# Sync-queue loads moved behind the transposes, and fewer small VectorE instructions, in a latent-attention layer

## The chip, the cores and the metric

The kernel runs on one core of one Trainium2 chip. The metric is the device time of one execution in microseconds (us). The core has a matrix engine (TensorE, PE in the profile, with its weight loads as PEld), a vector engine (VectorE, DVE), an activation engine (ScalarE, ACT), GpSimd (POOL) and a sync engine (SyncE, SP) which in this kernel issues every DMA. Engines run their own instruction lists in order and wait for each other on counting semaphores.

## The reference

Input x is 2048 rows by 512. The layer is `x + attention(xn) + ffn(xn)`, where `xn` is x after a layer norm.

```
q = xn @ wq                          # 16 heads of 128 + 64 (rotary)
kva = xn @ wkv_a                     # 128 latent + 64 rotary columns
ckv = rmsnorm(kva[:, :128]) * kv_norm_scale
k_nope, v = split(ckv @ wkv_b)       # 16 heads of 128 and 128
q_pe, k_pe = rope(q_pe), rope(k_pe)  # one k_pe for all heads
scores = (q_nope . k_nope + q_pe . k_pe) * 192 ** -0.5, causal
out = softmax(scores) @ v @ wo
ffn = sum over 8 factors of xn @ factors[r], / sqrt(8), + bias
```

## The kernel before

Weights are absorbed: for a head, `wq` and the key part of `wkv_b` are multiplied once (`w_abs`, stored to DRAM), and so are the value part of `wkv_b` and `wo` (`w_vo`), so that scores are taken against the 128 latent columns and a head's output is one product more. Operands are split into a high and a low float16 part, and each product is three matmuls (high by high, high by low, low by high). The high part is a ScalarE copy and the low part a difference made on VectorE or GpSimd.

After a prologue (layer norm, transposes of x, latent keys; up to about 71 us of the profile) the work goes by units. A unit `i` is one head for one chunk of 512 query rows: 64 units, 16 heads for each of the chunks 3, 2, 1, 0 in this order, and two more rounds for what trails. A unit has four rows `r` of 128 queries, and a row has `chunk + 1` pieces of at most 512 keys, so each of units 0 to 15 has 16 pieces. All five instruction lists walk the same loops. For each piece:

- TensorE makes the scores (L534 to L540) in one of four PSUM banks. It may write a bank when ScalarE's exponential of four pieces before has read it.
- VectorE takes the maximum (L1123, L1125). After the row's last piece `row_max` makes the bias of the exponentials: L1135, then L1142, which computes `m * scale + head` in a `tensor_scalar` with two per-partition operands.
- ScalarE makes the exponential (L774, `exps`) and then a float16 copy of it, the high part (L784, `high_parts`).
- GpSimd makes the low part (L1341), and SP transposes both with one DMA (L1513).
- One unit later TensorE multiplies them by the latent values (L390 to L392).

Behind each row's pieces every engine does the row's `fills(i, r)`: the next unit's query, outputs of the unit before the last, and, in units 0 to 15 only, the weight work of heads to come. Of this weight work the following matters here.

- `load_wo(i)` (L1419) fills `wso`, which has one buffer. It is read by ScalarE's `sqo` fill of unit i at row 3 (L752, sum of squares). TensorE sums that over partitions (L439, fill `nv`) in unit i + 1, row 0, and VectorE's `scale_value` makes scales of the sum.
- `load_wq(i + 4)` (L1401) fills one of two buffers `wsq`, and `load_wk(i + 5)` (L1407) one of four buffers `wsk`. In odd units ScalarE squares both query weights of the pair i + 3, i + 4: `sq0` at row 2 and `sq1` at row 3 (L695). `sq1(i + 3)` therefore reads the `wsq` that `load_wq(i + 4)` fills in the same unit. TensorE's fill `nrm(i + 3)` (L439) comes in unit i + 1, row 0, behind `nv`, and waits for `sq1`. VectorE's `scale_pair` reads that.

The order on SP is written by hand in the loop at L1545. Within a unit at row 2 it is: `load_wo`, `load_wk`, `load_wq`; the row's transposes; `load_factor` (L1443, in units 1 to 7; in unit 0 four loads of L1438); `load_pe`. Rows 0, 1 and 3 have their transposes first and other loads and stores behind them. A transpose waits for GpSimd's low part of its piece.

In unit 0 alone, ScalarE's order is all exponentials of a row and then all its copies (L784). In the other units a copy follows each exponential but the first, one piece behind.

Of the kernel before, what the change touches and what calls it, by code (L numbers as in the profile page):

```python
# [6 lines left out]
F32, F32R = mybir.dt.float32, mybir.dt.float32r  # L7
# [5 lines left out]
P = 128  # L13
# [191 lines left out]
def build(nc, x, wq, wkv_a, wkv_b, wo, kvs, factors, bias, rope_t, rope_n, out):  # L205
    ctx = ExitStack()
    with ctx:
        def sb(name, shape, dt):
            return ctx.enter_context(nc.sbuf_tensor(name, shape, dt))
# [29 lines left out]
        nrf = sb("nrf", [P, KE], F32)  # L239
        lat = sb("lat", [P, 6], F32)  # L240
        fsc = sb("fsc", [P, 5], F32)
# [134 lines left out]
        def pair(i):  # L376

            return i % H // 2
# [259 lines left out]
        def _(e):  # L638
# [223 lines left out]
            for i in range(NU + 2):  # L862
                for r in range(QT):
                    last = chunk(i) if i < NU else -1

                    soon = last == 0 and r == 3 and i % 2
                    for kind, n in fills(i, r):
                        if soon and kind == "pv":
                            fill(kind, n)
                    for p in range(last + 1):  # L870
                        exps(i, r, p)

                        if p and i:
                            high_parts(i, r, p - 1)
                        if p == 2 and r < 2:

                            for kind, n in fills(i, r):
                                if kind in ("q", "wo", "parts", "sqv"):
                                    fill(kind, n)
                    for p in range(0 if i == 0 else max(last, 0), last + 1):  # L880
                        high_parts(i, r, p)
                    for kind, n in fills(i, r):
                        if soon and kind == "pv":
                            continue
                        if last < 2 or r >= 2 or kind not in ("q", "wo", "parts", "sqv"):
                            fill(kind, n)
# [3 lines left out]
        def _(e):  # L890
# [18 lines left out]
            def root(y, n):  # L909

                return e.tensor_scalar(y.bitcast(I32), n.bitcast(I32), -0.5, ROOT, ALU.mult, ALU.add)
# [4 lines left out]
            def scale_pair(i):  # L916
# [8 lines left out]
                e.wait_ge(z["v_fourth"], i // 2 + 1)  # L925
                e.tensor_scalar(t[:, 1:2], t[:, 2:3], lat[:, 4:5], None, ALU.add).then_inc(z["v_prod"], 1)
                root(t[:, 3:4], t[:, 0:1])
                e.wait_ge(z["v_prod"], i // 2 + 1)
                root(t[:, 4:5], t[:, 1:2]).then_inc(z["v_root"], 1)
                e.wait_ge(z["v_root"], i // 2 + 1)  # L930
                e.tensor_scalar(t[:, 5:6], t[:, 3:4], t[:, 4:5], None, ALU.mult)
                e.tensor_scalar(sc[:, 0:1], t[:, 3:4], WS, None, ALU.mult)
                e.tensor_scalar(sc[:, 1:2], t[:, 4:5], WS, None, ALU.mult).then_inc(z["v_w2"], 1)
                e.wait_ge(z["v_w2"], i // 2 + 1)
                e.reciprocal(t[:, 6:7], t[:, 5:6]).then_inc(z["v_inv"], 1)
                e.tensor_scalar(sc[:, 4:5], t[:, 5:6], lat[:, 5:6], None, ALU.mult).then_inc(z["v_tau"], 1)
                e.wait_ge(z["v_inv"], i // 2 + 1)
# [4 lines left out]
            def scale_value(h):  # L942
# [10 lines left out]
                e.wait_ge(z["v_nv"], h + 1)  # L953
                root(t[:, 2:3], t[:, 0:1])
                root(t[:, 3:4], t[:, 1:2]).then_inc(z["v_vroot"], 1)
                e.wait_ge(z["v_vroot"], h + 1)
                e.tensor_scalar(t[:, 4:5], t[:, 2:3], t[:, 3:4], None, ALU.mult)
                e.tensor_scalar(sc[:, 0:1], t[:, 2:3], WS, None, ALU.mult)
                e.tensor_scalar(sc[:, 1:2], t[:, 3:4], WS, None, ALU.mult).then_inc(z["v_vw"], 1)
                e.wait_ge(z["v_vw"], h + 1)  # L960
                e.reciprocal(sc[:, 2:3], t[:, 4:5]).then_inc(z["v_vsc"], 1)

            def scale_latent():
# [10 lines left out]
                e.reciprocal(lat[:, 2:3], lat[:, 3:4]).then_inc(z["v_lat"], 1)  # L974
                e.wait_ge(z["v_lat"], 1)
                e.tensor_scalar(lat[:, 5:6], lat[:, 2:3], WS * KS / RS, None, ALU.mult).then_inc(z["v_lat"], 1)

# [150 lines left out]
            def row_max(i, r):  # L1128
# [10 lines left out]
                if i < H and r == 0:  # L1139
                    e.wait_ge(z["v_scale"], i // 2 + 1)  # L1140

                e.tensor_scalar(nm[:, R % 4:R % 4 + 1], m, scales[:, pair(i), 3:4], head[:, 0:1], ALU.mult,  # L1142
                                ALU.add).then_inc(z["v_nm"], 1)

# [240 lines left out]
        def _(e):  # L1385
# [159 lines left out]
            for i in range(NU + 2):  # L1545
                k, h = divmod(i, H)
                for r in range(QT):
                    if r == 2:
                        if 1 <= i < H:
                            load_wo(i)  # L1550
                        if i + 5 < H:
                            load_wk(i + 5)
                        if i + 4 < H:
                            load_wq(i + 4)
                    if i < NU:
# [21 lines left out]
                    if 1 <= i and KE + (i - 1) * QT + r + 2 < NF:  # L1577
                        load_factor(KE + (i - 1) * QT + r + 2)
                    if r == 2 and i % 2 and H <= i + 3 < NU:
                        load_pe(i + 3)  # L1580
                    if r == 1 and h == H - 3 and k + 1 < NC:
# [48 lines left out]
```

## Time and profile before

| | |
|---|---|
| median of 3 runs | 1529.21 us (1527.36 to 1529.43) |
| time of the profiled execution | 1529.43 us |
| its span, first to last instruction | 1527.5 us |
| TensorE busy | 1479.1 us, 97% |
| VectorE, ScalarE, GpSimd busy | 66%, 64%, 59% |
| DMA engines of the core, moved | 73% busy, 226 MB on the one hardware queue |
| mean granted TensorE clock | 0.994 of full speed |

Times in the profile count from the first instruction of the span. The profiled execution took 1.9 us more than its span.

### The profile page before, as it was taken

The page shows a single profiled execution, that of the slowest core. Times are in us where ns is not written, and L with a number is a line of the kernel's source. Part 1 is how long each engine was busy: PE and PEld are TensorE (multiplying, and loading weights), DVE is VectorE, ACT ScalarE, POOL GpSimd, SP SyncE. Part 2 cuts the span into 40 slices and gives each one's busy share as a digit, 9 for nine tenths or more (in the row PEclk, how much of TensorE's full clock was granted, in tenths as well). Part 3 has the DMA queues.
Part 4 walks back from the last instruction along what each step waited for, and adds up shares of the span by engine and source line. Part 5 has one row for each costly group of instructions (what it writes and reads, how often), then busy time and mean ns, then how long its engine had stood idle before and what let it go on. Part 6 is the DMA issues. An engine that isn't in the chain of part 4 may idle for free.

```text
span 1527.5 us, 25754 instructions
## 1 busy us (share of the span) xinstructions
PE 1479.1 (97%) x7908; PEld 758.3 (50%) x7908; DVE 1012.5 (66%) x2563; ACT 974.4 (64%) x2418; POOL 904.7 (59%) x905
## 2 busy tenths in 40 slices
PE   5789999999999999999999999999999999999997
PEld 4444455555544544444445454545545555455553
DVE  6666777767777766655455565656656666676786
ACT  6777676777767476666466667665646666654553
POOL 1367777775655455666465656566645655664552
PEclk9999999999999999999999999999999999999998
DMA  6369989998776588787677677886856677854654
GB/s 219 105 124 206 205 181 189 187 189 163 150 154 139 114 174 168 142 175 138 131 143 139 134 139 146 153 162 134 155 117 138 136 140 149 157 133 98 120 119 99
DMA packets 646598, 227.83 MB, mean 149 GB/s; under 512 B 599360, under 2 KB 612160, under 8 KB 646080
## 3 DMA queue, kind: packets, MB, share of 16 engines
q1 hardware_dynamic: 646464, 226.20, 73.0%
q8 instruction: 65, 1.06, 0.3%
q14 instruction: 69, 0.57, 0.1%
HBM read 65.67 MB, written 17.83 MB: 55 GB/s over the span
## 4 chain that ended last, share of the span: by engine, by line
PE 80%; ACT 7%; DVE 6%; issue 3%; POOL 3%; DMA 1%; SPq 0%; POOLq 0%; ACTq 0%; DVEq 0%
PE ps L390 16%; PE ps L391 16%; PE ps L392 16%; PE ps L534 6%; PE ps L539 6%; PE ps L540 6%; PE ps L536 6%; PE ps L535 6%; ACT ex L774 3%; POOL st L1341 1%; DVE gm L1123 1%; DVE ps L1125 1%; POOL q L1332 1%; DMA st<-x_in 0%; ACT sqr L695 0%
## 5 line engine op out<-in xcount | busy, mean ns | idle before, releaser
L1341 POOL TENSOR_TENSOR st<-ex,st 128x512 f16<-128x512 f32 (+3 forms) x640 | 637.7, 1015 | 504.3 <-ACT st L784 494.5
L774 ACT ACTIVATE ex<-ps,nm,scales 128x512 f32<-128x512 f32 (+3 forms) x640 | 452.5, 709 | 466.8 <-DVE nm L1142 452.8
L1123 DVE TENSOR_REDUCE gm<-ps 128x1 f32<-128x512 f32 (+1 forms) x384 | 249.0, 669 | 176.8 <-PE ps L540 172.6
L784 ACT ACTIVATE st<-ex 128x512 f16<-128x512 f32 (+3 forms) x640 | 341.4, 561 | 5.9
L534 PE MATMUL ps<-kTh,q 128*128 128x512 f16 (+3 forms) x640 | 223.2, 349 | 8.5 <-ACT ex L774 8.4
L539 PE MATMUL ps<-kRh,q 128*128 128x512 f16 (+3 forms) x640 | 222.9, 348 | 4.5 <-POOL q L1332 4.5
L390 PE MATMUL ps<-pT,vH 128*128 128x512 f16 (+3 forms) x640 | 222.4, 347 | 2.4 <-DMA pT<-st 2.4
L536 PE MATMUL ps<-kTh,q 128*128 128x512 f16 (+3 forms) x640 | 223.0, 348 | 0.0
L535 PE MATMUL ps<-kTl,q 128*128 128x512 f16 (+3 forms) x640 | 223.0, 348 | 0.0
L540 PE MATMUL ps<-kRl,q 128*128 128x512 f16 (+3 forms) x640 | 223.0, 348 | 0.0
L391 PE MATMUL ps<-pT,vH 128*128 128x512 f16 (+3 forms) x640 | 222.5, 348 | 0.0
L392 PE MATMUL ps<-pT,vL 128*128 128x512 f16 (+3 forms) x640 | 219.3, 348 | 0.0
L1176 DVE SCALAR_TENSOR_TENSOR acc<-ps,rden,acc 128x512 f32<-128x512 f32 x256 | 189.7, 743 | 4.1 <-PE ps L392 3.7
L1332 POOL TENSOR_TENSOR q<-rot,q 32x512 f16<-32x512 f32 x128 | 149.0, 1164 | 28.6 <-ACT q L763 16.5
L1125 DVE CUSTOM_DVE_ANT_0 ps<-ps,cmask 128x256 f32<-128x256 f32 (+3 forms) x256 | 133.0, 519 | 26.1 <-PE ps L540 23.4
L774 ACT ACTIVATION_READ_ACCUMULATOR ex<-ps,nm,scales 128x1 f32 x640 | 125.7, 196 | 0.0
L1100 DVE SCALAR_TENSOR_TENSOR q<-ps,q 128x512 f16<-128x512 f32 x64 | 44.2, 691 | 114.6 <-ACT q L757 114.6
L390 PE MATMUL ps<-wV,oT 128*128 128x512 f16 x256 | 97.7, 382 | 4.7 <-issue 3.1
L534 PEld LDWEIGHTS ps<-kTh,q 128*128 128x128 f16 x640 | 62.7, 98 | 77.9 <-ACT ex L774 16.8
L391 PE MATMUL ps<-wV,oT 128*128 128x512 f16 x256 | 97.7, 382 | 0.0
L392 PE MATMUL ps<-wV,oT 128*128 128x512 f16 x256 | 97.7, 382 | 0.0
L390 PE MATMUL ps<-xT,wA 128*128 128x512 f16 x256 | 97.0, 379 | 0.0
(200 smaller groups left out, 2145.2 us busy)
## 6 DMA issues: line engine op xcount, KB each, us to landing
wA<-w_abs SPq DMA_DIRECT2D x48, 256.0 KB, 3.0
wV<-w_vo SPq DMA_DIRECT2D x48, 256.0 KB, 3.0
pT<-st SPq DMA_TRANSPOSE x640, 3.3
fland<-factors_in SPq DMA_DIRECT2D x28, 256.0 KB, 3.3
wP<-w_pe SPq DMA_DIRECT2D x24, 256.0 KB, 3.0
wsq<-wq_in SPq DMA_DIRECT2D x16, 256.0 KB, 3.9
wso<-wo_in SPq DMA_DIRECT2D x16, 256.0 KB, 3.1
w_abs<-wA SPq DMA_DIRECT2D x16, 256.0 KB, 2.3
```

Of the source, the lines that this page charges most:

```text
L390: e.matmul(o, a[0], b[0], start=first, stop=False)
L391: e.matmul(o, a[0], b[1], start=False, stop=False)
L392: return e.matmul(o, a[1], b[0], start=False, stop=last)
L534: e.matmul(b, q[:, i % 2, 0, qs], kTh[:, ks], start=True, stop=False)
L535: e.matmul(b, q[:, i % 2, 0, qs], kTl[:, ks], start=False, stop=False)
L536: e.matmul(b, q[:, i % 2, 1, qs], kTh[:, ks], start=False, stop=False)
L539: e.matmul(b, q[:, i % 2, 2, qs], kRh[:, ks], start=False, stop=False)
L540: e.matmul(b, q[:, i % 2, 2, qs], kRl[:, ks], start=False, stop=True).then_inc(z["p_s"], 1)
L774: e.activation(ex[:, n % NEX, 0:keys], s_bank(n)[:, 0:keys], ACT.Exp, bias=nm[:, (i * QT + r) % 4:(i * QT + r) % 4 + 1], scale=scales[:, p ...
L784: e.activation(stage(n, keys)[:, :, 0, :], ex[:, n % NEX, 0:keys].rearrange("p (t n) -> p t n", n=P), ACT.Copy).then_inc(z["a_pH"], 1)
L1123: e.tensor_reduce(m, b, AX_X, ALU.max).then_inc(z["v_max"], 1)
L1341: e.tensor_tensor(s[:, :, 1, :], ex[:, n % NEX, 0:keys].rearrange("p (t n) -> p t n", n=P), s[:, :, 0, :], ALU.subtract).then_inc(z["g_pL" ...
```

## The change

It has three parts.

1. SP: at row 2 of a unit, `load_wo`, `load_wk` and `load_wq` are issued behind the row's transposes and behind `load_factor`, no longer ahead of the transposes. `load_pe` keeps its place in the order.
2. ScalarE, unit 0: each high part is made one piece behind its exponential, as in the other units.
3. VectorE: in `scale_pair` and `scale_value` two operations on neighbouring columns become one on two columns, and operations with a per-partition scalar operand become ones between two tensors; `row_max` uses `scalar_tensor_tensor`, with one per-partition scalar operand and a tensor, where it used two scalar operands. One column of `lat` and its operation go.

```diff
@@ ScalarE
                         exps(i, r, p)
-                        if p and i:
+                        if p:
                             high_parts(i, r, p - 1)
...
-                    for p in range(0 if i == 0 else max(last, 0), last + 1):
-                        high_parts(i, r, p)
+                    if last >= 0:
+                        high_parts(i, r, last)
@@ scale_pair
-                e.tensor_scalar(t[:, 1:2], t[:, 2:3], lat[:, 4:5], None, ALU.add).then_inc(z["v_prod"], 1)
-                root(t[:, 3:4], t[:, 0:1])
+                e.tensor_tensor(t[:, 1:2], t[:, 2:3], lat[:, 4:5], ALU.add).then_inc(z["v_prod"], 1)
                 e.wait_ge(z["v_prod"], i // 2 + 1)
-                root(t[:, 4:5], t[:, 1:2]).then_inc(z["v_root"], 1)
+                root(t[:, 3:5], t[:, 0:2]).then_inc(z["v_root"], 1)
                 e.wait_ge(z["v_root"], i // 2 + 1)
-                e.tensor_scalar(t[:, 5:6], t[:, 3:4], t[:, 4:5], None, ALU.mult)
-                e.tensor_scalar(sc[:, 0:1], t[:, 3:4], WS, None, ALU.mult)
-                e.tensor_scalar(sc[:, 1:2], t[:, 4:5], WS, None, ALU.mult).then_inc(z["v_w2"], 1)
+                e.tensor_tensor(t[:, 5:6], t[:, 3:4], t[:, 4:5], ALU.mult)
+                e.tensor_scalar(sc[:, 0:2], t[:, 3:5], WS, None, ALU.mult).then_inc(z["v_w2"], 1)
...
-                e.tensor_scalar(sc[:, 4:5], t[:, 5:6], lat[:, 5:6], None, ALU.mult).then_inc(z["v_tau"], 1)
+                e.scalar_tensor_tensor(out=sc[:, 4:5], in0=t[:, 5:6], scalar=WS * KS / RS, in1=lat[:, 2:3],
+                                       op0=ALU.mult, op1=ALU.mult).then_inc(z["v_tau"], 1)
@@ scale_value
-                root(t[:, 2:3], t[:, 0:1])
-                root(t[:, 3:4], t[:, 1:2]).then_inc(z["v_vroot"], 1)
+                root(t[:, 2:4], t[:, 0:2]).then_inc(z["v_vroot"], 1)
                 e.wait_ge(z["v_vroot"], h + 1)
-                e.tensor_scalar(t[:, 4:5], t[:, 2:3], t[:, 3:4], None, ALU.mult)
-                e.tensor_scalar(sc[:, 0:1], t[:, 2:3], WS, None, ALU.mult)
-                e.tensor_scalar(sc[:, 1:2], t[:, 3:4], WS, None, ALU.mult).then_inc(z["v_vw"], 1)
+                e.tensor_tensor(t[:, 4:5], t[:, 2:3], t[:, 3:4], ALU.mult)
+                e.tensor_scalar(sc[:, 0:2], t[:, 2:4], WS, None, ALU.mult).then_inc(z["v_vw"], 1)
@@ row_max
-                e.tensor_scalar(nm[:, R % 4:R % 4 + 1], m, scales[:, pair(i), 3:4], head[:, 0:1], ALU.mult,
-                                ALU.add).then_inc(z["v_nm"], 1)
+                e.scalar_tensor_tensor(out=nm[:, R % 4:R % 4 + 1], in0=m, scalar=scales[:, pair(i), 3:4], in1=head[:, 0:1],
+                                       op0=ALU.mult, op1=ALU.add).then_inc(z["v_nm"], 1)
@@ SP
                 for r in range(QT):
-                    if r == 2:
-                        if 1 <= i < H:
-                            load_wo(i)
-                        if i + 5 < H:
-                            load_wk(i + 5)
-                        if i + 4 < H:
-                            load_wq(i + 4)
                     if i < NU:
                         for p in range(chunk(i) + 1):
                             transpose(i, r, p)
...
                     if 1 <= i and KE + (i - 1) * QT + r + 2 < NF:
                         load_factor(KE + (i - 1) * QT + r + 2)
-                    if r == 2 and i % 2 and H <= i + 3 < NU:
-                        load_pe(i + 3)
+                    if r == 2:
+                        if 1 <= i < H:
+                            load_wo(i)
+                        if i + 5 < H:
+                            load_wk(i + 5)
+                        if i + 4 < H:
+                            load_wq(i + 4)
+                        if i % 2 and H <= i + 3 < NU:
+                            load_pe(i + 3)
```

## Rows read from the trace of the kernel before

**Rows 1.** The page's busy time, share of the span and instructions of TensorE.

```profile
PE 1479.1 (97%) x7908; PEld 758.3 (50%) x7908; DVE 1012.5 (66%) x2563; ACT 974.4 (64%) x2418; POOL 904.7 (59%) x905
```

**Rows 2.** Windows: length, each engine's busy time, granted clock, DMA share, GB/s.

```profile
100.00:500.00 400.00, 396.29 (x2120) 200.78 (x2119) 292.94 (x752) 292.43 (x738) 282.07 (x269) 1.00 0.89 178
500.00:1500.00 1000.00, 998.32 (x5249) 502.87 (x5247) 640.07 (x1584) 603.59 (x1475) 586.08 (x578) 1.00 0.71 140
1500.00:1528.00 28.00, 17.36 (x85) 7.96 (x83) 14.90 (x35) 7.68 (x18) 5.12 (x6) 0.86 0.41 98
```

**Rows 3.** Waits of TensorE from 100 to 500 us: in total, times, longest.

```profile
PE ps L534 <- ACT ex L774: 3.5, 8, 0.9
```

**Rows 4.** Timeline of TensorE: the two longest of those waits, in brackets.

```profile
121.52 0.34 PE L534 MATMUL ps<-kTh,q 128*128 128x384 f16 x1 [0.68 <-ACT ex L774]
...
154.03 0.34 PE L534 MATMUL ps<-kTh,q 128*128 128x384 f16 x1 [0.92 <-ACT ex L774]
```

**Rows 5.** Timeline of SP, units 0 and 1: start, time in issuing.

```profile
100.11 0.39 SPq L1401 DMA_DIRECT2D wsq<-wq_in  x1
102.16 5.35 SPq L1513 DMA_TRANSPOSE pT<-st  x4
...
133.74 0.58 SPq L1443 DMA_DIRECT2D fland<-factors_in  x1
134.37 0.43 SPq L1419 DMA_DIRECT2D wso<-wo_in  x1
...
135.37 0.38 SPq L1401 DMA_DIRECT2D wsq<-wq_in  x1
135.80 5.58 SPq L1513 DMA_TRANSPOSE pT<-st  x4
```

**Rows 6.** Timeline of GpSimd: the low parts of unit 1, row 2.

```profile
131.29 4.26 POOL L1341 TENSOR_TENSOR st<-ex,st 128x512 f16<-128x512 f32 x4
```

**Rows 7.** DMA issues, us to landing: `wsq` of unit 1, then of unit 4.

```profile
wsq<-wq_in SPq DMA_DIRECT2D x1, 256.0 KB, 3.4
...
wsq<-wq_in SPq DMA_DIRECT2D x1, 256.0 KB, 4.7
```

**Rows 8.** Timeline of ScalarE: `sqo(1)` and `sq1(4)`, unit 1, row 3.

```profile
138.73 0.63 ACT L752 ACTIVATE sqs<-wso 128x512 bf16<-128x512 f32 x1
...
139.35 0.62 ACT L695 ACTIVATE sqr<-wsq 128x512 bf16<-128x512 f32 x1
139.87 0.20 ACT L695 ACTIVATION_READ_ACCUMULATOR sqr<-wsq 128x1 f32 x1
```

**Rows 9.** Timeline of TensorE: the product `nrm(4)`, unit 2, row 0.

```profile
140.38 0.36 PE L439 MATMUL ps<-nrm,ones 128*128 128x4 f32 x2
```

**Rows 10.** Timeline of TensorE: two waits in unit 0.

```profile
75.17 0.39 PE L539 MATMUL ps<-kRh,q 128*128 128x512 f16 x1 [3.01 <-POOL q L1332]
...
96.06 0.39 PE L534 MATMUL ps<-kTh,q 128*128 128x512 f16 x1 [1.60 <-ACT ex L774]
```

**Rows 11.** Windows behind those two waits, columns as in rows 2.

```profile
75.00:81.00 6.00, 4.72 (x17) 2.14 (x17) 2.86 (x7) 1.69 (x4) 0.12 (x1) 0.72 0.00 0
94.00:100.00 6.00, 4.40 (x28) 2.11 (x26) 5.54 (x11) 5.53 (x13) 5.70 (x6) 1.00 0.89 122
```

**Rows 12.** Small VectorE instructions by shape: count, busy us, mean ns, idle before.

```profile
L1142 DVE TENSOR_SCALAR nm<-rm,scales,head 128x1 f32<-128x1 f32 x192 | 52.4, 273 | 7.5 <-DVE rm L1135 0.6
...
L926 DVE TENSOR_SCALAR tot<-tot,lat 128x1 f32<-128x1 f32 x8 | 1.7, 214 | 0.3
L906 DVE SCALAR_TENSOR_TENSOR rstd<-mv,rstd 128x2 f32<-128x2 f32 x8 | 1.3, 160 | 0.3
...
L932 DVE TENSOR_SCALAR scales<-tot 128x1 f32<-128x1 f32 x8 | 1.1, 143 | 0.0
```

**Rows 13.** Timeline of unit 5: SP's transposes at row 2, `sq1(8)`, `nrm(8)`.

```profile
265.24 5.99 SPq L1513 DMA_TRANSPOSE pT<-st  x4
...
275.29 0.63 ACT L695 ACTIVATE sqr<-wsq 128x512 bf16<-128x512 f32 x1
...
277.11 0.36 PE L439 MATMUL ps<-nrm,ones 128*128 128x4 f32 x2
```

More of the change, by code:

```diff
@@ L239, in build @@
         nrf = sb("nrf", [P, KE], F32)
-        lat = sb("lat", [P, 6], F32)
+        lat = sb("lat", [P, 5], F32)
         fsc = sb("fsc", [P, 5], F32)
@@ L974, in scale_latent @@
                 e.reciprocal(lat[:, 2:3], lat[:, 3:4]).then_inc(z["v_lat"], 1)
-                e.wait_ge(z["v_lat"], 1)
-                e.tensor_scalar(lat[:, 5:6], lat[:, 2:3], WS * KS / RS, None, ALU.mult).then_inc(z["v_lat"], 1)
             def scale_factors():
```

## The prediction

> **What bounds the kernel now.** I read the page's busy times first. TensorE is busy 1479 of 1527.5 us [rows 1], so no other engine's time counts unless TensorE waits for it. The windows say where the 48 us that it isn't busy lie [rows 2]: 3.7 us between 100 and 500 us (most of units 0 to 15, in which the weight work is done), 1.7 us between 500 and 1500, 10.6 us at the end, and the rest, 32 us, ahead of 100 us. The waits of TensorE between 100 and 500 us are of one kind, for an exponential: 3.5 us in eight waits [rows 3]; the two longest are 0.68 and 0.92 us, one in unit 1 and one in unit 2 [rows 4]. The six others share 3.5 - 1.6 = 1.9 us. So the change can win little there, and what decides is whether it makes TensorE wait for something new.
>
> **Loads behind the transposes.** Issuing is slow on SP: four transposes take it 5.3 to 6.0 us [rows 5, 13], and a plain load of 256 KB some 0.4 to 0.6 us. In unit 1 SP is late: it goes from one transfer to the next without a pause from 133.74 to 141.38 us, while GpSimd's low parts of that row run from 131.29 to 135.55 us [rows 5, 6]. Here the moved loads lose the whole time of the row's transposes and of a factor load. Step by step, for `load_wq(5)`:
>
> - SP is done with the factor load of row 1 at 133.74 + 0.58 = 134.3 us. In the changed kernel it may be there sooner. In unit 0 it sits idle from 100.50 to 102.16 us with the next transposes waiting for GpSimd [rows 5], while two loads that now go behind are already out; and the earlier copies of unit 0 (below) bring the data sooner. Nothing shows how much comes of it: between 0 and 1.7 us. I take the middle, 0.9, and 133.4 us.
> - Four transposes, 5.6 us [rows 5]: 139.0. GpSimd is not in the way, its last low part is done at 135.6 [rows 6].
> - A factor load, 0.6, then `wso` and `wsk` at about 0.5 each: `wsq` is issued at 140.6 instead of 135.37.
> - It lands 3.4 us later as in unit 1 before, or 4.7 as in unit 4 [rows 7]. The transposes just ahead of it are still in flight, so I take 4.0: 144.6 us.
>
> Who waits? ScalarE reads it at 139.35 us for `sq1(4)` and needs 0.72 us to the end of it [rows 8]; now it ends at 145.3. Behind `sq1(4)` on ScalarE stand all the exponentials of unit 2. TensorE wants `sq1(4)` for `nrm(4)` at 140.38 us [rows 9], and behind that stand an output product and the scores of unit 2, row 1. So TensorE stops for about 4.9 us, nearly all of it lost, since nothing else is ready in its order. `wso`, issued 1 us sooner, lands and is squared before `wsq` is there and adds nothing. Bounds from the same rows: 133.4 - 0.8 and landing 3.4 give +3.5 us; no advance and landing 4.7 give +6.5 us.
>
> **The clock.** After the 3.01 us wait in unit 0 TensorE ran at the lower of its two levels (1.2 GHz instead of 2.4) for part of what followed: over 6 us the granted clock was 0.72, so 6 x 0.28 = 1.7 us of full-speed work were lost. After a wait of 1.60 us it stayed 1.00 [rows 10, 11]. A wait of 5 us is more like the first: +1.7 us, bounds 0 and 1.7.
>
> The Trainium skill, "TensorE: Matmul & The Clock Gate", Part 1, says that the gate halves the clock when the array has been idle and that the moment depends on a phase which runs free of the kernel, so it can fall otherwise from run to run. By it both 0 and 1.7 us are possible, and the row gives the likelier.
>
> **Later odd units.** Units 3, 5, 7, 9, 11 load a `wsq` that is read in the same unit, but there SP is not late. In unit 5 the transposes end at 271.23 us [rows 13]. Without three loads ahead of them they can start up to 1.4 us sooner; I take 0.9, as GpSimd holds them back. Then 270.3 + 0.6 + 1.0 = 271.9 for `wsq`, landing 275.3 to 276.6, and `sq1(8)` ends 0.72 later, 276.0 to 277.3. ScalarE wanted the data at 275.29, TensorE the sum at 277.11 [rows 13]. So ScalarE idles 0 to 1.3 us and TensorE 0 to 0.2. ScalarE's lateness goes into the exponentials and the query copy of the next unit, whose waits on TensorE are the small ones of [rows 3]. From unit 8 on there is no factor load, and it is nothing. In even units only `wso` is late, and `nv` comes late enough on TensorE. With TensorE set back by unit 1, SP has caught up by unit 2.
>
> **VectorE's small instructions.** L1142 takes 273 ns with two per-partition operands, L926 214 with one, L932 143 with none [rows 12]: some 65 ns each. A `scalar_tensor_tensor` with one such operand isn't in this trace at that size; L906, with a constant and two tensors, takes 160 [rows 12]. So the new L1142 lies between 160 and 273 ns; nearest is 160 plus one operand, 214 to 225. I take 214: 59 ns a row, 256 x 59 ns = 15 us of VectorE, all of it beside a busy TensorE, and 0.06 us on the path to an exponential where one is waited for. `scale_pair` loses two operations of 143 ns, of which I count half, since neighbours without a wait between them overlap, and about 0.06 three times: 0.3 us (bounds 0 and 0.5). `scale_value` likewise 0.2. These stand ahead of the maxima in rows 0 and 1, and so in the chain that ends the waits of [rows 3]: up to 0.5 us for an even unit, 0.25 for an odd one. Of the 1.9 us of the six small waits I take 1.0 back, the rest being eaten by the late `sq1`. The 0.92 us wait of unit 2 goes whole, for TensorE comes there later than the exponentials do: it lost 4.9 + 1.7, they lost 4.9 less 0.5. The 0.68 us of unit 1 may shrink, but lies ahead of the new stop, whose end SP sets; so a gain there, or in the prologue or unit 0, only makes the stop longer, and counts nothing.
>
> **Unit 0's copies.** They put one copy in front of the third exponential of a row and two in front of the fourth. TensorE's waits there end with the first exponential of a row [rows 10], which they leave alone. Bounds -0.3 and +0.5 us; whatever it is, the stop in unit 1 swallows it, apart from SP's advance above. If that stop isn't there, they are worth about -0.2.
>
> **The sum**, against the profiled execution's own 1529.4 us (0.2 above the median, at the top of the three runs): stop +4.9, clock +1.7, wait of unit 2 -0.9, small waits -1.0. That is +4.7, and 1534.1 us. The end of the kernel, 10.6 us of idle, has two rows of L1142 in its chain at most, -0.1, which I leave out.
>
> **The rivals.**
>
> - A, the loads are hidden anyway, and the kernel isn't slower. It needs `wsq` in place by 139.7 us, so the issue done by about 136, where 140.6 is my figure. It decides if the four transposes take SP 1 us in place of 5.6, or SP comes 5 us sooner. The Trainium skill, "DMA: Bandwidth & Descriptors", Issuing engines are not separate DMA queues, calls the issuing time usually small beside the transfer, which speaks for A. The rows speak against it: 5.58 us of issuing for four, back to back. What A gives: -0.9 -1.9 -0.2 and some 0.3 of the 0.68, 1526.1 at best; with half of it, 1528.
> - B, as forecast, but the clock keeps its level: the wait of unit 2 then shrinks by 0.5 only, +4.9 - 0.5 - 1.0 = +3.4, 1532.8.
> - C, the lateness repeats: in units 3, 5 and 7 `wsq` lands at the slow end or beyond. Each then costs 0.2 of TensorE's own waiting and up to 1.3 through late exponentials, and the 1.0 isn't won: +1.0 + 3 x 1.0 = 4 us more, 1538. For it: the DMA engines are 89% busy [rows 2]. Against it: landings in 3.4 to 4.7 us already under that load.
> - D, partly hidden: SP is 2 us or more ahead by unit 1 and the landing is short. +2 us, no clock loss, 1530.5.
>
> **Chances.** Forecast 0.46, B 0.14, C 0.16, A 0.13, D 0.11. A measurement of this kernel tells about 0.2%, 3 us, from no change. Slower: forecast and C whole, B for the most part: 0.71. Same: D, most of A, the rest of B: 0.23. Faster: a part of A with gains in the prologue that I don't see: 0.06. The range takes in B, D and most of C: 1529.5 to 1539. The likeliest case's own is 1532.5 to 1536.
>
> **What would show it.** Right: `wsq<-wq_in` issued at about 140 to 141 us in unit 1; ScalarE idle some 5 us around 139 to 144 us, ended by a landing; TensorE's L439 with an idle of 4 us or more ahead of it, with the clock below 1.00 in the window behind; no wait of 0.9 us in unit 2; L1142's successor near 214 ns. Wrong: TensorE's idle between 100 and 500 us unchanged or less (A); idles ahead of the L439 of units 4, 6 and 8 too (C).

## The result, and the profile after

| | before | after |
|---|---|---|
| median | 1528.39 us (1527.36 to 1529.43, 4 runs) | 1547.27 us (1544.82 to 1548.66, 4 runs) |
| profiled execution: time, span | 1529.43, 1527.5 us | 1548.28, 1546.4 us |

The ratio is 1.0129, interval 1.0116 to 1.0142. The change costs 19 us, not 5, and the time lies above the forecast's range.

The page's busy times after, against [rows 1]:

```profile
PE 1480.9 (96%) x7908; PEld 755.3 (49%) x7908; DVE 1070.7 (69%) x2514; ACT 972.5 (63%) x2418; POOL 903.3 (58%) x905
```

The first surprise stands here: VectorE runs 49 instructions fewer and is busy 58.2 us longer. The windows after, with the columns of [rows 2]:

```profile
100.00:500.00 400.00, 385.31 (x2041) 193.58 (x2040) 312.52 (x684) 283.57 (x718) 271.79 (x260) 0.99 0.86 172
500.00:1500.00 1000.00, 995.31 (x5214) 499.63 (x5213) 661.57 (x1563) 599.63 (x1468) 580.81 (x572) 1.00 0.70 140
```

TensorE is idle 14.7 us between 100 and 500 us (before 3.7) and 4.7 between 500 and 1500 (before 1.7). Its waits from 100 to 500 us, against [rows 3]:

```profile
PE ps L534 <- ACT ex L774: 9.8, 13, 1.5
PE ps L439 <- ACT sqs L752: 2.8, 1, 2.8
PE ps L390 <- DVE q L1094: 1.2, 1, 1.2
PE ps L439 <- ACT sqr L695: 0.6, 1, 0.6
```

Two of the four kinds are the stop that was forecast, 2.8 + 0.6 us. The largest, for an exponential, has grown from 3.5 to 9.8 us, and nothing in the forecast did that.

**The stop in unit 1.** The timelines of SP, ScalarE and TensorE after, against [rows 5, 8, 9]:

```profile
133.26 5.34 SPq L1506 DMA_TRANSPOSE pT<-st  x4
...
139.27 0.43 SPq L1412 DMA_DIRECT2D wso<-wo_in  x1
...
140.27 0.38 SPq L1394 DMA_DIRECT2D wsq<-wq_in  x1
```

```profile
142.48 0.63 ACT L752 ACTIVATE sqs<-wso 128x512 bf16<-128x512 f32 x1 [3.45 <-DMA wso<-wo_in]
...
143.56 0.63 ACT L695 ACTIVATE sqr<-wsq 128x512 bf16<-128x512 f32 x1 [0.36 <-DMA wsq<-wq_in]
```

```profile
143.35 0.56 PE L439 MATMUL ps<-nv,ones 128*128 128x2 f32 x2 [2.76 <-ACT sqs L752]
144.54 0.56 PE L439 MATMUL ps<-nrm,ones 128*128 128x4 f32 x2 [0.64 <-ACT sqr L695]
```

Read them from top to bottom: SP issues four transposes first, then both loads; ScalarE stands until each has landed, and TensorE stands for ScalarE. The trace books 2.76 us on `wso` and 0.64 on `wsq`, because `nv` comes ahead of `nrm` in TensorE's order; the end of the stop is set by `wsq`. In the window behind it the clock is at its lower level throughout:

```profile
144.00:150.00 6.00, 5.46 (x14) 2.22 (x15) 3.37 (x12) 5.24 (x15) 3.30 (x4) 0.50 1.00 228
```

**VectorE's small instructions.** The groups by shape after, against [rows 12]:

```profile
L1135 DVE SCALAR_TENSOR_TENSOR nm<-rm,scales,head 128x1 f32<-128x1 f32 x192 | 83.5, 435 | 7.3 <-DVE rm L1129 0.6
...
L1135 DVE SCALAR_TENSOR_TENSOR nm<-gm,scales,head 128x1 f32<-128x1 f32 x64 | 34.7, 542 | 2.3
...
L925 DVE TENSOR_TENSOR tot<-tot,lat 128x1 f32<-128x1 f32 x8 | 6.3, 790 | 0.3
...
L929 DVE TENSOR_TENSOR tot<-tot 128x1 f32<-128x1 f32 x8 | 4.3, 543 | 0.3
L910 DVE TENSOR_SCALAR tot<-tot 128x2 int32<-128x2 int32 x8 | 4.0, 494 | 0.3
```

`row_max`'s new form (L1135) was to take 214 ns and takes 435 and 542 on average; with 118.2 us it has 48.3 of the 58.2 us more (69.9 before). The average hides two populations. These are the listings of tile `nm`, before and after (shortest, median and longest in ns):

```profile
L1142 DVE TENSOR_SCALAR nm<-rm,scales,head x192: 272/273/276, 80.7 to 1323.5; 128x1 f32<-128x1 f32 x192
L1142 DVE TENSOR_SCALAR nm<-gm,scales,head x64: 272/273/275, 1327.1 to 1505.6; 128x1 f32<-128x1 f32 x64
```

```profile
L1135 DVE SCALAR_TENSOR_TENSOR nm<-rm,scales,head x192: 218/220/1235, 80.7 to 1339.4; 128x1 f32<-128x1 f32 x192
L1135 DVE SCALAR_TENSOR_TENSOR nm<-gm,scales,head x64: 218/318/1277, 1343.4 to 1525.7; 128x1 f32<-128x1 f32 x64
```

The old form takes the same 272 to 276 ns each time. The new one takes 218 ns at best, which is what the forecast had, and up to 1277. The timelines show what stretches such an instruction. Here is `scale_pair` in unit 4, on GpSimd, VectorE, ScalarE and TensorE:

```profile
219.65 1.54 POOL L1334 TENSOR_TENSOR st<-ex,st 128x384 f16<-128x384 f32 x2 [0.29 <-ACT st L784]
221.15 1.27 POOL L1266 TENSOR_TENSOR fsum<-fsum,fland 128x512 f32<-128x512 f32 x1
```

```profile
219.69 0.89 DVE L925 TENSOR_TENSOR tot<-tot,lat 128x1 f32<-128x1 f32 x1
220.62 0.60 DVE L910 TENSOR_SCALAR tot<-tot 128x2 int32<-128x2 int32 x1
221.25 1.18 DVE L929 TENSOR_TENSOR tot<-tot 128x1 f32<-128x1 f32 x1
222.36 0.15 DVE L930 TENSOR_SCALAR scales<-tot 128x2 f32<-128x2 f32 x1
```

```profile
225.63 0.78 ACT L774 ACTIVATE ex<-ps,nm,scales 128x512 f32<-128x512 f32 x1 [5.75 <-DVE nm L1135]
```

```profile
226.55 0.39 PE L534 MATMUL ps<-kTh,q 128*128 128x512 f16 x1 [1.53 <-ACT ex L774]
```

L929 ends at 222.43 us, and GpSimd's instruction at 222.42; L910 ends at 221.22 us, GpSimd's two low parts at 221.19. L925 ends at 220.58 us, the first of the two low parts at 220.56. Three instructions of some 160 ns took 2.67 us, each to the end of what GpSimd was doing, and L930, which runs as GpSimd stops, took 0.15. From the start of L925 to that of the bias L1135 it is 5.7 us; in the kernel before the same stretch takes 3.6. So the exponential comes 2.0 us later, and TensorE waits 1.53 us.

The kernel before has this effect too, in an instruction that the change leaves alone. This is the listing of tile `rden` in the kernel before (shortest, median and longest in ns):

```profile
L1155 DVE SCALAR_TENSOR_TENSOR rden<-rtmp,vsc x64: 161/163/1221, 133.0 to 1513.1; 128x4 f32<-128x4 f32 x64
```

Two tensors in SBUF, 163 ns mostly, once 1221. Of the 64, 60 took 161 to 222 ns and four 591, 593, 986 and 1221; each of these four began beside a working GpSimd and ended 16 to 18 ns behind the end of GpSimd's instruction. The forecast didn't read it.

### The profile page after: what moved, and what is told of

Same layout as the page of the kernel before. It is cut to its first block, busy times and chain, and to the rows that moved or that the text cites. A ratio compares the mean times of both kernels' runs of the same rounds, so it can differ in the third digit from the quotient of the medians.

```text
span 1546.4 us, 25705 instructions
## 1 busy us (share of the span) xinstructions
PE 1480.9 (96%) x7908; PEld 755.3 (49%) x7908; DVE 1070.7 (69%) x2514; ACT 972.5 (63%) x2418; POOL 903.3 (58%) x905
## 4 chain that ended last, share of the span: by engine, by line
PE 72%; DVE 10%; ACT 8%; issue 6%; POOL 2%; DMA 1%; SPq 0%; ACTq 0%; POOLq 0%; DVEq 0%
PE ps L390 14%; PE ps L391 14%; PE ps L392 14%; PE ps L534 6%; PE ps L539 6%; PE ps L540 6%; PE ps L536 6%; PE ps L535 6%; ACT ex L774 4%; DVE ps L1119 2%; DVE gm L1117 1%; DVE acc L1169 1%; POOL st L1334 1%; DVE nm L1135 1%; ACT q L757 1%
## 5 line engine op out<-in xcount | busy, mean ns | idle before, releaser
L534 PE MATMUL ps<-kTh,q 128*128 128x512 f16 (+3 forms) x640 | 223.2, 349 | 15.9 <-ACT ex L774 15.6
```

What stands on the lines that cost most here:

```text
L534: e.matmul(b, q[:, i % 2, 0, qs], kTh[:, ks], start=True, stop=False)
```

## The experiments

All ratios are to the kernel before on the same chip. "Lag" is by how much the first score matmul of a unit comes later than in the kernel before, read from the two traces; the last column is the last score matmul of all.

| run | median, us | ratio, interval | lag at unit 3 | 11 | 32 | end |
|---|---|---|---|---|---|---|
| the whole change | 1547.27 | 1.0129, 1.0116 to 1.0142 | 6.2 | 15.1 | 15.6 | 19.3 |
| e1_loads | 1535.29 | 1.0049, 1.0036 to 1.0063 | 7.2 | 7.6 | 7.6 | 7.6 |
| e2_vector | 1544.48 | 1.0107, 1.0094 to 1.0121 | 1.7 | 10.9 | 11.4 | 15.1 |
| e3_rowmax | 1535.79 | 1.0047, 1.0034 to 1.0059 | 2.3 | 4.2 | 4.5 | 8.4 |
| e4_scales | 1540.01 | 1.0075, 1.0061 to 1.0088 | 5.9 | 13.4 | 13.6 | 13.6 |
| e5_copies | 1526.11 | 0.9989, 0.9981 to 0.9998 | -0.9 | -0.9 | -0.9 | -0.9 |
| e6_oneinput | 1532.26 | 1.0031, 1.0020 to 1.0042 | 6.0 | 6.2 | 5.8 | 5.7 |
| e7_headimm | 1525.68 | 0.9987, 0.9978 to 0.9996 | 0.2 | -0.4 | -0.7 | -0.9 |
| e8_ex1 | 1530.74 | 1.0019, 1.0010 to 1.0028 | 2.5 | 2.7 | 2.6 | 2.6 |
| e12_pairs | 1534.62 | 1.0039, 1.0025 to 1.0053 | 0.1 | 4.2 | 4.4 | 4.4 |
| e9_best | 1524.26 | 0.9978, 0.9969 to 0.9987 | -1.7 | -2.1 | -2.5 | -2.6 |

The ratios rest on all executions, a lag on one of each kernel, and TensorE's clock differs from one to the next where it has just waited. From 74 to 92 us the granted clock was 0.81 in the kernel before and 0.91 in e12_pairs, which is 3.4 and 1.6 us not granted; in the last 28 us it was 0.86 in the kernel before and 1.00 in e1_loads. So a lag and the difference of the medians can part by 2 to 3 us.

**e1_loads: part 1 alone.** The SP hunk of the change, nothing else.

> The kernel before with the loads moved behind the transposes, and nothing else of the change. Theory (two causes: the late loads cost one stop in unit 1, and VectorE's new instructions cost the rest): TensorE stops about 3.4 us ahead of nv(1) and nrm(4), then runs some 3 us worth of work at the lower clock; the score matmuls from unit 3 on are 5 to 7 us later than before and stay so, 1534 us. Rival 1 (the loads carry all of it, through lateness in all odd units): +15 us or more, the lag growing at units 4, 6, 8, 10. Rival 2 (VectorE alone carries it): within 1 us of before.

All of its lag is there at unit 3 and none is added later. Waits of TensorE around the stop:

```profile
PE ps L439 <- ACT sqs L752: 4.2, 1, 4.2
...
PE ps L439 <- ACT sqr L695: 0.8, 1, 0.8
```

That is 5.0 us of stop against 3.4 in the whole change. SP is later here: `wso` is issued at 141.65 us, with the whole change at 139.27. The time, 1535.3 us, is near the 1534 expected.

**e2_vector: part 3 alone.** The hunks of `scale_pair`, `scale_value` and `row_max`.

> The kernel before with all of VectorE's new instructions, and nothing else. Theory: the lag grows by about 2 us at each of units 4, 6, 8 and 10, behind scale_pair, and by some 3 to 4 us in the last 500 us: +11 to +13 us, 1540 us. Rival 1 (loads carry all): within 1 us of before or up to 2 us faster. Rival 2 (VectorE alone): +19 us.

1.0107, or 16.4 us, is 3 to 5 us more than expected. So this part is the larger one, and the sign of its forecast (a gain of 1 us or so) was wrong. The two that follow divide it.

**e3_rowmax: `row_max`'s form alone.**

```diff
-                e.tensor_scalar(nm[...], m, scales[:, pair(i), 3:4], head[:, 0:1], ALU.mult, ALU.add)
+                e.scalar_tensor_tensor(out=nm[...], in0=m, scalar=scales[:, pair(i), 3:4], in1=head[:, 0:1],
+                                       op0=ALU.mult, op1=ALU.add)
```

> The kernel before with the new form in row_max alone (256 instructions). Theory: its mean goes from 273 to about 460 ns, most of it beside a busy TensorE; what shows is the last 500 us and a part of units 0 to 15, +4 us, 1532 to 1534. If the cost lay in this instruction alone, +11 or more. VectorE busy +48 us.

It costs 7.2 us, where about 4 were expected. The mean was 446 ns (x192) and 543 (x64), and the lag comes in two places: 4.2 us in units 0 to 11, and from 4.9 to 8.4 in units 48 to 63, where a row has one piece. That the bias is a larger part of the chain there is a reading, not shown; half of that growth, 1.8 us, comes in unit 50 alone.

**e4_scales: `scale_pair` and `scale_value` alone.**

> The kernel before with the new scale_pair and scale_value alone. Theory: only 24 short chains, but each scale_pair is 1 to 2 us longer and stands ahead of the maxima of an even unit's rows: +5 to +8 us, all of it gained by unit 12, 1535 us. VectorE busy +9 us. Rival (only the 256 instructions of row_max count): within 1 us of before.

It costs 11.5 us, where 5 to 8 were expected. Its lag grows in units 2 to 11 and stops when the last pair's scales are made. From unit 2 to unit 3 it goes from 0.3 to 5.9 us, and that is one place, which VectorE, GpSimd and TensorE show so:

```profile
141.97 6.77 DVE L911 TENSOR_SCALAR vtot<-vtot 128x2 int32<-128x2 int32 x1
```

```profile
139.15 3.38 POOL L1336 TENSOR_TENSOR st<-ex,st 128x512 f16<-128x512 f32 x3
142.50 1.26 POOL L1268 TENSOR_TENSOR fsum<-fsum,fland 128x512 f32<-128x512 f32 x1
143.73 3.76 POOL L1336 TENSOR_TENSOR st<-ex,st 128x512 f16<-128x512 f32 x4
147.46 1.25 POOL L1268 TENSOR_TENSOR fsum<-fsum,fland 128x512 f32<-128x512 f32 x1
```

```profile
150.57 1.08 PE L414 MATMUL ps<-ident,wsq 128*128 128x128 f32 x4 [3.81 <-DVE q L1095]
```

One instruction on two columns stood for 6.77 us, over the GpSimd instruction that it began in and six more, until GpSimd paused at 148.71 us. TensorE waited 3.81 us and lost 1.7 to the clock behind it (0.72 over the 6 us from 150). No other small instruction of the five traces of before, e2, e3, e4 and after took longer than 1.29 us.

**e6_oneinput: the whole change, with other VectorE forms.** `scale_pair`, `scale_value` and `row_max` are written so that each instruction reads one SBUF tensor of one column; loads and copies are as in the whole change:

```diff
-                e.scalar_tensor_tensor(out=nm[...], in0=m, scalar=scales[:, pair(i), 3:4], in1=head[:, 0:1], ...)
+                e.tensor_scalar(nm[...], m, scales[:, pair(i), 3:4], HEADROOM, ALU.mult, ALU.add)
...
-                e.tensor_tensor(t[:, 1:2], t[:, 2:3], lat[:, 4:5], ALU.add)
+                e.tensor_scalar(t[:, 1:2], t[:, 2:3], lat[:, 4:5], None, ALU.add)
```

> The changed kernel with its loads behind the transposes and its unit 0 copies, but every VectorE operation that reads two SBUF tensors, or two columns in one tensor_scalar, given back a form with one SBUF tensor of one column and per-partition operands; row_max takes one per-partition operand and a constant. Theory (VectorE instructions with two SBUF inputs, and the two-column ones, wait for GpSimd's running instruction): VectorE's busy time falls to about 1000 us (before: 1012; after: 1070), what is left is the moved loads, 1529 + 4 to 6 us: 1532 to 1535. Rival (the new forms cost the same and the loss is from the number or the order of the VectorE operations and its coupling with the late loads): 1543 to 1547.

VectorE's busy time and the form of `row_max`:

```profile
PE 1476.1 (96%) x7908; PEld 756.8 (49%) x7908; DVE 999.2 (65%) x2562; ACT 973.7 (64%) x2418; POOL 903.6 (59%) x905
```

```profile
L1139 DVE TENSOR_SCALAR nm<-rm,scales 128x1 f32<-128x1 f32 x192 | 41.1, 214 | 6.9
```

1.0031: all but 4.7 us of the loss is gone, and the loads are still late. Three quarters of what the change costs is the form of a few VectorE instructions. VectorE runs 48 instructions more here than in the whole change and is busy 71.5 us less. `row_max`'s form is that of e7_headimm below, which is itself cheaper than the old one.

**e7_headimm: the kernel before with `head` as a constant.** One line, as in e6.

> The kernel before with one thing changed: row_max adds a constant where it added the per-partition operand head, so it is a tensor_scalar with one per-partition operand and one SBUF tensor. This is what the prediction priced the new form at: 214 ns in place of 273, 256 times, 15 us of VectorE. Expected: mean 205 to 220 ns, VectorE busy 997, and time 1526.5 to 1528.5 (the prediction's small gains of 1.0 us or less). Rival: the mean of this form too rises when GpSimd works (over 300 ns), and the time goes up as with the scalar_tensor_tensor form (+7.5 us).

214 ns, and 0.9987: 2.0 us less (interval 0.6 to 3.4), where 1 us at most was expected. 214 ns is the price that the forecast gave the new form; a form of that price exists, but it isn't the one in the change.

**e5_copies: part 2 alone.** The ScalarE hunk.

> The kernel before with part 2 alone: in unit 0 each high part one piece behind its exponential. Loads moved alone and loads moved with the rest differ in where SP stands in unit 1: wso was issued at 141.65 us with the loads alone and at 139.27 us with the whole change. If the copies are what brings SP there sooner, then here SP issues the factor load, wso and wsq of unit 1 some 2 us ahead of the kernel before (wsq near 133.4 us instead of 135.37), and the time stays within 1 us of it (1527.5 to 1529.5), because no load is late in that order. Rival: the copies do nothing to SP and the 2.4 us come from VectorE's new forms; then wsq is issued at 135 us here. The prediction gave the copies alone -0.2 us.

`wsq` of unit 1 is issued at 134.05 us in place of 135.37, so the copies do bring SP there sooner, by 1.3 us. That is less than the 2 us expected. The time is 1.7 us less (interval 0.3 to 2.9), a little more than the 1 us that was allowed for; the trace shows 0.7 of it as the wait of 0.68 us in unit 1 [rows 4], which is gone.

**e8_ex1: the loads behind the transposes everywhere but in unit 1.**

```diff
-                    if r == 2:
+                    if r == 2 and i == 1:
                         load_wo(i)
...
                     if i < NU:
                         for p in range(chunk(i) + 1):
                             transpose(i, r, p)
...
+                    if r == 2 and i != 1:
+                        if 1 <= i < H:
+                            load_wo(i)
```

> The kernel before with part 1 in every unit but unit 1, which keeps its loads ahead of the transposes. The loads alone cost 7.0 us, and the trace of that run showed its lag at 7.2 us behind unit 1 and flat from there. If unit 1 is the only stop (the prediction's place for it), this is within 1.5 us of the kernel before: 1526.5 to 1529.5. Rival C of the prediction (the lateness repeats in units 3, 5 and 7, hidden in the other run only because unit 1 had set TensorE back already): then a stop shows in unit 3 or 5 and the time is 1531 or more.

No stop in units 3, 5 or 7: the lag is flat from unit 2 on. ScalarE waits 0.52 us for `wso` in unit 2 and 0.05 us for `wsq` in unit 3, and TensorE doesn't feel it. But the time, 1530.74 us, lies above the expected 1526.5 to 1529.5: 2.7 us arise before unit 2, at a place that nobody had named, a wait for a transposed piece:

```profile
116.17 0.59 PE L390 MATMUL ps<-pT,vH 128*128 128x512 f16 x1 [2.02 <-DMA pT<-st]
```

The 2.7 us are this wait and 1.7 us not granted by the clock behind it, less the 0.68 us wait of unit 1 [rows 4], which is gone here.

In unit 0 the late `wsk` and `wsq` are issued between the transposes of row 2 and those of row 3, which begin at 110.35 us (before 109.60) and end at 117.57 (before 115.65). In the whole change the copies have SP there 2.6 us sooner (107.76 us), and this wait isn't in its trace. That the copies cover it isn't shown, though: e6_oneinput has them too, with SP there at 107.75 us, and waits 1.07 us at this place; e1_loads, which has unit 0 as here and no copies, waits 0.65. With the same order the four transposes took SP 5.99 us in e1_loads and 7.22 here; why is open.

**e12_pairs: only the merges of two columns, each with one SBUF tensor.**

```diff
-                root(t[:, 3:4], t[:, 0:1])
                 e.wait_ge(z["v_prod"], i // 2 + 1)
-                root(t[:, 4:5], t[:, 1:2]).then_inc(z["v_root"], 1)
+                root(t[:, 3:5], t[:, 0:2]).then_inc(z["v_root"], 1)
...
-                e.tensor_scalar(sc[:, 0:1], t[:, 3:4], WS, None, ALU.mult)
-                e.tensor_scalar(sc[:, 1:2], t[:, 4:5], WS, None, ALU.mult).then_inc(z["v_w2"], 1)
+                e.tensor_scalar(sc[:, 0:2], t[:, 3:5], WS, None, ALU.mult).then_inc(z["v_w2"], 1)
```

> The kernel before with only the merges of two columns into one tensor_scalar in scale_pair and scale_value (four instructions of a pair of units become two, twice); each reads one SBUF tensor. Prediction: -0.3 to -0.5 us in all. Theory that the two-column form is held too, as in the separate measurement (163 ns beside an idle GpSimd, 1117 ns beside a working one): up to 1 us more in front of the maxima of row 0 or 1 of a unit, of which the 16 weight units have 24 instances with two such instructions each: +2 to +8 us, part of the 11.7 us that scale_pair and scale_value cost together. Rival (the loss is from the forms with two tensors alone): within 1 us of before.

```profile
L955 DVE TENSOR_SCALAR vsc<-vtot 128x2 f32<-128x2 f32 x16 | 5.0, 311 | 0.0
...
L911 DVE TENSOR_SCALAR tot<-tot 128x2 int32<-128x2 int32 x8 | 4.5, 565 | 0.3
```

Two columns in one instruction instead of two instructions of one column cost 6 us, half of what e4_scales does. The lag of 4.4 us understates it by the clock in unit 0. The merge also puts the wait for `v_prod` ahead of both roots; e6_oneinput and e9_best have it there too and are the faster ones, so it isn't the wait.

**e11_probe: seven forms by themselves.** VectorE starts each of them while GpSimd does one thing or another; the layer is left out. Its core:

```
tensor_reduce(filler, ps[:, 0:64]) -> GpSimd starts;  tensor_reduce(filler, ps[:, 0:256])
L50 tensor_scalar(o, s, t, u)            two per-partition operands
L52 scalar_tensor_tensor(o, s, t, u)     two SBUF tensors, one operand
L54 tensor_tensor(o, s, t)               two SBUF tensors
L56 tensor_scalar(o, s, t, 0.5)          one operand
L58 tensor_scalar(o, s, 0.5)             one column
L60 tensor_scalar(o, s[:, 0:2], 0.5)     two columns
L62 scalar_tensor_tensor(o, ps, t, u)    one tensor in PSUM, one in SBUF
```

> A measurement of VectorE's small forms by themselves; the whole layer is left out and x is copied to the output, so its time says nothing of the kernel. Seven forms on 128x1 operands, 12 times each, beside GpSimd doing (phase 0) a 1-column memset, (1) one 128x512 float32 tensor_tensor, (2) four of them back to back, (3) one 128x512 memset that reads nothing. Theory (two SBUF inputs wait for GpSimd): in phases 1 and 2 the scalar_tensor_tensor with both tensors in SBUF, the tensor_tensor and perhaps the two-column tensor_scalar take about 1 us or more, the others what they take in phase 0: 273 ns with two per-partition operands, 214 with one, 143 with none; with four back to back the held ones end with the first or with the last of the four, which tells how the 6.77 us of one instruction came about; with a memset nothing is held; the scalar_tensor_tensor with one tensor in PSUM isn't held. Rival (the forms are slow in themselves): they take as long in phase 0 as in phase 1.

Groups by shape beside one 128x512 tensor_tensor of GpSimd, then two groups beside its one-column memset:

```profile
L60 DVE TENSOR_SCALAR o<-s 128x2 f32<-128x2 f32 x12 | 13.4, 1118 | 0.0
L54 DVE TENSOR_TENSOR o<-s,t 128x1 f32<-128x1 f32 x12 | 13.3, 1108 | 0.0
L52 DVE SCALAR_TENSOR_TENSOR o<-s,t,u 128x1 f32<-128x1 f32 x12 | 13.3, 1107 | 0.0
L50 DVE TENSOR_SCALAR o<-s,t,u 128x1 f32<-128x1 f32 x12 | 3.2, 266 | 0.0
L62 DVE SCALAR_TENSOR_TENSOR o<-ps,t,u 128x1 f32<-128x1 f32 x12 | 2.5, 209 | 0.0
L56 DVE TENSOR_SCALAR o<-s,t 128x1 f32<-128x1 f32 x12 | 2.5, 204 | 0.0
L58 DVE TENSOR_SCALAR o<-s 128x1 f32<-128x1 f32 x12 | 1.7, 144 | 0.0
```

```profile
L52 DVE SCALAR_TENSOR_TENSOR o<-s,t,u 128x1 f32<-128x1 f32 x12 | 2.6, 214 | 0.0
...
L60 DVE TENSOR_SCALAR o<-s 128x2 f32<-128x2 f32 x12 | 2.0, 163 | 0.0
```

Three forms are held and four are not, with no exception in twelve. A per-partition operand counts as no second tensor, nor does a tensor in PSUM. The rival (slow in themselves) falls: 214 and 163 ns with GpSimd quiet. Beside four GpSimd instructions back to back the held forms take the same 1107 to 1117 ns: they get in behind the first. Beside a memset of 128x512, which reads nothing, the two with two inputs take their usual 210 and 150 ns, and only the two-column one is held, to 357 ns, where nothing was expected to be.

The Trainium skill, "SBUF — State Buffer", SBUF: two separate sides, has this rule: VectorE and GpSimd share one pair of SBUF ports, whoever starts first holds it for the whole instruction, and on VectorE's side that concerns instructions in a two-port mode, and those with two SBUF inputs against a GpSimd operation that reads SBUF. The rows agree as far as VectorE comes second: both kinds are held, to the end of one instruction, and the memset tells them apart. That two columns are a two-port mode is the page's reading, no row names the mode; no row here shows GpSimd held by VectorE; and the 6.77 us above go beyond one instruction. The rule was to be had before the forecast, and it is the rule that speaks against this change.

**e13_probe2: one start after another.** Five GpSimd instructions of 1151 ns back to back, and three forms (a tensor_tensor of one column, a tensor_scalar of two float32 and of two int32) begun after 28 different delays, four times each.

> A second measurement of VectorE's small forms by themselves (the whole layer is left out, x is copied to the output). GpSimd does five float16 = float32 - float16 tensor_tensors of 128x512 back to back; VectorE starts a 128x1 tensor_tensor, a two-column float32 and a two-column int32 tensor_scalar after 28 different delays in steps of about 50 ns, 4 times each. Open is how one instruction of the run with the new scales alone could be held 6.77 us, across six GpSimd instructions. If a held instruction gets in at the end of the running one, every duration is the rest of that one, at most 1.15 us, wherever it starts. If one that starts in some stretch of it misses its turn, some durations are 1.2 to 2.3 us or more, and the delay or the form says where; if only the int32 form does, it is the form.

In 324 of 336 cases (in the other 12 the instruction began ahead of GpSimd's and took 148 to 159 ns) it ended 14 to 26 ns behind the end of the GpSimd instruction that it had begun in. None crossed into the next. So the 6.77 us of e4_scales stay unexplained: neither back-to-back instructions nor the int32 form bring it about by themselves.

**e9_best: what the runs point to.** The loads where they were, part 2 of the change, and `row_max` with the constant. As in e6_oneinput, the one column of `lat` and its operation are gone too, and a wait of `scale_pair` stands one instruction earlier.

> What the runs so far point to: the kernel before with its loads where they were, the unit 0 copies one piece behind (alone 0.9989 of before), row_max with one per-partition operand and a constant (alone 0.9987), and L1155's product of two SBUF tensors replaced so that it reads one. If the two gains add, 0.9976 of before, 1524 us; if they are taken from the same small waits, 1525.5 to 1526.5. It is not slower than before under either theory of the VectorE forms; over 1529 would say that the gains of the single edits were chance.

The expectation names a change of L1155's product as well; the kernel that ran leaves it as it was. 0.9978: 3.4 us faster than before, about the sum of 1.7 and 2.0 for its two main edits.

## Why the prediction was wrong

The direction was right and for a reason that holds, but it explains a quarter to a third of the loss: 4.7 us in e6_oneinput, and in the trace of the whole change 3.4 us of stop and 3.1 of clock. By its own steps:

- **The step that failed: "So the new L1142 lies between 160 and 273 ns; nearest is 160 plus one operand".** L906, the row taken as nearest [rows 12], has two SBUF inputs as the new form does, but its 8 instances lie in the prologue, and GpSimd stands still at every one of them. L1155, whose 64 instances lie in the stretch where GpSimd works, with 1221 ns at the longest, was nearer. Measured: 435 and 542 ns. The same step lets `scale_pair` and `scale_value` gain 0.3 and 0.2 us by having fewer instructions; measured, part 3 costs 16.4 us (e2_vector), of which `row_max` has 7.2 and the scales 11.5 when each is alone. The bound "below 273" had no row of two SBUF inputs behind it that was taken with GpSimd at work.
- **"All of it beside a busy TensorE"** holds for most of `row_max`'s time and not for the rest: of the 50 us more that VectorE is busy with it in e3_rowmax, 7.2 reach the time, and of the 15 us less in e7_headimm, 2.0. In the whole change the waits for an exponential from 100 to 500 us grow from 3.5 to 9.8 us.
- **The stop in unit 1: right in place and mechanism.** Transposes ended 138.6 us (139.0 said), `wsq` issued at 140.27 (140.6), landing 3.3 us (4.0), stop 3.40 us (4.9, bounds 3.5 to 6.5, so a little below the lower one). SP's advance was said to be 0.9 us, from the copies; alone they give 1.3.
- **The clock: a term too small.** After the stop TensorE ran at the level of 1.2 GHz from 143.35 to 150.16 us, and was busy 6.17 us of it: half of that, 3.1 us, was lost, where 1.7 was both the value and the upper bound. In e1_loads the clock fell while TensorE still stood; from 145.74 to 150.70 us it was busy 4.18 us at that level and lost 2.1. One row of a 3.01 us wait was no bound for this: behind the same wait of unit 0 the granted clock was 0.72 over 75 to 81 us in the kernel before [rows 11], 0.50 in e7_headimm (3.0 us not granted) and 1.00 in e2_vector. The Trainium skill, "TensorE: Matmul & The Clock Gate", Part 1, has the halving begin at a phase that is not the kernel's; by that no single window gives a bound. The three agree with it. Behind the 2.02 us wait of e8_ex1 1.7 us were not granted (0.83 and 0.88 over the 6 us from 112 and from 118), and nothing behind the 1.53 us at 226.55 (1.00 from 226 to 232 us).
- **The 0.92 us wait of unit 2** didn't go whole: 0.36 us were left at 160.24 us.
- **Later odd units** cost nothing: in e1_loads, e6_oneinput and e8_ex1 ScalarE waits at most 0.52 us for a late load behind unit 1, and TensorE never for that. Rival C falls, with one reserve: in each of these runs TensorE was 2.5 us or more late by unit 3, so odd units without any earlier lateness weren't measured. Unit 0's late loads weren't looked at; they gave TensorE a wait of 0 to 2.02 us (the whole change, 0.65 in e1_loads, 1.07 in e6_oneinput, 2.02 in e8_ex1).
- **The copies** were said to be worth 0.2 us without the stop, and are worth 1.7 (interval 0.3 to 2.9).

For the loads, the copies and the form that was priced, the sum was good: e6_oneinput has just these, and 1.0031 x 1529.2 = 1533.9 us against the 1534.1 forecast. Its parts were off in both directions, though (stop too large, clock too small, copies and form worth more), so that is partly luck. The rest is 1.0129 / 1.0031 = 1.0098, 15 us, for instructions that are held, against forms of which one, that of `row_max`, is itself 2.0 us better than the old one. Added up, the parts alone give 1.0049 + 0.0107 - 0.0011 = 1.0145; the 1.0129 of the whole differs by no more than the intervals leave open.

What stays open is the one instruction held for 6.77 us. It cost e4_scales 3.8 + 1.7 = 5.5 us in its profiled execution. Whether it comes in every execution isn't shown. That run's five times spread from 1536.54 to 1541.89 us, but their mean granted clocks differ too, 0.998 to 0.995, and 0.003 of 1540 us is 4.6 us; that is an estimate of what the clock alone could make of the spread.

## What to carry to other kernels

On VectorE, count what an instruction reads from SBUF before counting instructions: beside a busy GpSimd two instructions with one SBUF tensor of one column (144 ns each) beat one with two tensors or two columns (up to the rest of GpSimd's instruction, 1.1 us in the measurement and 1.28 at most in the whole change). Keep per-row constants as per-partition operands or, better, immediates. To price a form that the trace doesn't have, look for the row with the same kinds of inputs at a place with the same neighbours at work, and read its longest instance, not its mean. And when loads are moved behind other issues on a queue, ask it of every unit, the first one too.

## What the runs showed of the hardware

- A tensor_scalar on 128x2 is held like a two-input instruction (float32 1118 ns in e11_probe; float32 and int32 in every case of e13_probe2 that began in a GpSimd instruction), and the float32 one by a GpSimd memset as well (357 ns); on 128x1 it is not (144 ns).
- Each per-partition operand costs some 60 ns at this size: 144, 204 and 266 ns for none, one and two.
- A held instruction ends 14 to 26 ns behind GpSimd's, in 324 of 324 cases; once, in a full kernel, one stood over six more GpSimd instructions (6.77 us).
- TensorE's clock behind one and the same wait of 3.01 us: granted 0.50, 0.72 and 1.00 over the next 6 us in three executions.
